# Softmax division folded into the turning of the tiles, output copies on ScalarE, and a new order of three products

## The reference

```python
# layer 2, per image
energy = jnp.einsum('bci,bcj->bij', q, k)
attention = jax.nn.softmax(energy, axis=-1)
out = jnp.einsum('bcj,bij->bci', v, attention)
out = gamma[0] * out + xf
# layer 3, per image: scores of theta and phi over sqrt(c)
attn = jax.nn.softmax(scores, axis=-1)
f = jnp.einsum('nab,nib->nia', attn, g)
f = jnp.einsum('nchw,dc->ndhw', f, conv_w)
# then batch norm of f over all images, and + x
```

## Time and profile before

| what | value |
|---|---|
| median of three runs | 5767.16 us (5764.43 to 5773.0) |
| the profiled execution | 5769.15 us, its span 5767.4 us |
| busy, TensorE | 4678.8 us (81%) |
| busy, VectorE | 5074.8 us (88%) |
| busy, ScalarE | 3719.5 us (64%) |
| busy, GpSimd | 4708.2 us (82%) |
| mean granted TensorE clock | 0.946 of full speed |

### The profile page before, as it was taken

One profiled execution on the slowest core, in us unless ns is written; L12 is line 12 of the kernel. 1 busy time (PEld: TensorE's weight loads), 2 busy tenths in 40 slices (PEclk: granted clock), 3 DMA queues, 4 the chain that ended last, 5 costly groups with the idle time before them and its releaser, 6 DMA issues.

```text
span 5767.4 us, 61917 instructions
## 1 busy us (share of the span) xinstructions
PE 4678.8 (81%) x17331; PEld 2709.8 (47%) x17331; DVE 5074.8 (88%) x5978; ACT 3719.5 (64%) x6077; POOL 4708.2 (82%) x3342
## 2 busy tenths in 40 slices
PE   6568888888888888888888888888888888888771
PEld 6134454445445444544454454445444544544451
DVE  4699999999999999999999999999999999999933
ACT  3466666667666766666666667666666766666633
POOL 0698888898888889888988888888889888888810
PEclk9689999999999999999999999999999999999995
DMA  4465555555655555555655555655555555555527
GB/s 129 181 225 220 216 202 217 220 219 207 220 220 216 207 218 219 211 211 220 223 205 214 221 218 208 220 219 201 215 219 219 207 220 220 219 203 220 213 82 295
DMA packets 199100, 1216.87 MB, mean 211 GB/s; under 512 B 27881, under 2 KB 28657, under 8 KB 67697
## 3 DMA queue, kind: packets, MB, share of 16 engines
q1 hardware_dynamic: 194416, 1196.26, 56.1%
q10 hardware_dynamic: 4352, 16.78, 0.7%
HBM read 1158.43 MB, written 54.53 MB: 210 GB/s over the span
## 4 chain that ended last, share of the span: by engine, by line
PE 42%; DVE 25%; issue 15%; ACT 10%; POOL 6%; DMA 1%; DVEq 0%; SPq 0%; POOLq 0%; ACTq 0%
PE psA L814 14%; PE psE L814 13%; DVE psD L484 9%; DVE hs L488 8%; PE psT L814 6%; PE psT L987 4%; DVE nm L513 4%; ACT p L726 4%; POOL pa L300 3%; PE psY L814 3%; ACT da L680 2%; ACT L649 1%; ACT pt L690 1%; DVE psU L477 1%; POOL pa L306 1%
## 5 line engine op out<-in xcount | busy, mean ns | idle before, releaser
L300 POOL TENSOR_TENSOR pa<-hs,rows_all 128x1024 f32<-128x1024 f32 x1024 | 2411.4, 2355 | 530.6 <-DVE hs L488 529.6
L680 ACT ACTIVATE da<-delta,neg_a 128x512 f32<-128x512 f32 x2048 | 1380.2, 717 | 290.4 <-DVE hs L488 278.3
L484 DVE TENSOR_TENSOR psD<-rows_all,psU 128x512 f32<-128x512 f32 x2048 | 1415.1, 691 | 84.5 <-POOL hlast L304 6.2
L488 DVE TENSOR_TENSOR_SCAN hs<-da,hlast,psD 128x512 f32<-128x512 f32 x1024 | 1310.9, 1280 | 36.3
L306 POOL TENSOR_TENSOR pa<-pa 128x512 f32<-128x512 f32 x1024 | 1299.5, 1269 | 40.1
L488 DVE TENSOR_TENSOR_SCAN hs<-da,psD 128x512 f32<-128x512 f32 x1024 | 1249.5, 1220 | 35.2
L814 PE MATMUL psA<-pt,va 128*128 128x256 f32 x4096 | 947.4, 379 | 1.0 <-DVE x L531 0.6
L726 ACT ACTIVATE p<-psE,nm 128x1024 f32<-128x1024 f32 x512 | 571.2, 1116 | 493.4 <-DVE nm L513 493.4
L814 PEld LDWEIGHTS psA<-pt,va 128*128 128x128 f32 x4096 | 763.2, 190 | 178.8 <-issue 91.5
L513 DVE TENSOR_REDUCE nm<-psE 128x1 f32<-128x1024 f32 x512 | 618.7, 1208 | 216.5 <-PE psE L814 216.1
L690 ACT ACTIVATE pt<-psT 128x512 f32<-128x512 f32 x1024 | 559.0, 596 | 373.1 <-PE psT L987 361.6
(11 more groups left out here) (186 smaller groups left out, 5121.6 us busy)
## 6 DMA issues: line engine op xcount, KB each, us to landing
rows_all<-bc_scratch SPq DMA_DIRECT2D x1024, 1024.0 KB, 4.7
xin<-x SPq DMA_DIRECT2D x40, 512.0 KB, 7.7
xres<-x SPq DMA_DIRECT2D x64, 256.0 KB, 6.2
x_scratch<-x SPq DMA_DIRECT2D x32, 512.0 KB, 4.3
f_scratch<-fa SPq DMA_DIRECT2D x32, 512.0 KB, 6.8
xres<-x SPq DMA_DIRECT2D x8, 512.0 KB, 3.7
x1g<-x SPq DMA_DIRECT2D x8, 512.0 KB, 3.6
fa<-x SPq DMA_DIRECT2D x8, 512.0 KB, 3.6
```

The source lines that it names most:

```text
L300: pool.tensor_tensor(pa[:, k % PROD, :, :], hs[:, sl, :, :], rows_all[:, slot, 2:4, :], ALU.mult).then_inc(S["prod"], 1)
L484: dve.tensor_tensor(psD[:, :], rows_all[:, slot, j, :], psU[:, :], ALU.mult).then_inc(S["dbu_ok"], 1)
L488: dve.tensor_tensor_scan(hs[:, sl, j, :], da[:, sl, j, :], psD[:, :], hlast[:, h, n_:n_ + 1] if ch else 0.0, ALU.mult, ALU.add).then_inc(S ...
L680: act.activation(da[:, k % 2, j, :], delta[:, h, cols(ch)], ACT.Exp, scale=neg_a[:, h, 2 * q + j:2 * q + j + 1]).then_inc(S["da_ok"], 1)
```

## The change

The row sums are inverted tile by tile. ScalarE multiplies `ident` by the reciprocals into `spread`, a diagonal matrix (two buffers), and `turn` becomes 8 products of `p` with `spread` in place of 8 transposes, so that `pt` is already divided. The products with `rinv`, `rb` and VectorE's output work go. Gamma goes into the copy of `va` for m=0. For m=0 one more product per group, `ident` with `x1g`, adds the residual in `psA`. ScalarE copies the output from `psA` to `x2` or `fa`. On VectorE, `scans` is split in two, and the reciprocal stands between the second half's product and its scan. In `ORDER`, "rows" moves behind the energy of r=10 and "steps" ahead of that of r=11.

```diff
@@ -230,12 +230,15 @@
-        RECIP_AT = [10, 12, 15, 18]
+        RECIP_AT = [8, 9, 11, 12, 14, 15, 17, 18]
@@ -496,12 +504,12 @@
-                    for m, gq in groups_at(RECIP_AT, o):
-                        i = NG // 2 * m + gq
-                        pair = slice(GT * (i % 2), GT * (i % 2) + GT)
-                        wait(dve, "p_ok", a, GT * (i + 1))
-                        wait(dve, "av_mm", a, i - 1)
-                        dve.reciprocal(rinv[:, pair], rsum[:, pair]).then_inc(S["rinv_ok"], 1)
+                    for m, t in tiles_at(RECIP_AT, o):
+                        i = TILES * m + t
+                        sl = slice(i % (2 * GT), i % (2 * GT) + 1)
+                        wait(dve, "p_ok", a, i + 1)
+                        wait(dve, "spread_ok", a, i - 2 * GT + 1)
+                        dve.reciprocal(rinv[:, sl], rsum[:, sl]).then_inc(S["rinv_ok"], 1)
@@ -518,22 +526,7 @@
-                        wait(dve, "av_mm", a, i + 1)
-                        wait(dve, "rb_ok", a, i + 1)
-                        if m == 0:
...
-                            dve.scalar_tensor_tensor(out=psA[:, 0:GL], in0=psA[:, 0:GL], scalar=c_gam, in1=rb[:, :],
-                                                     op0=ALU.mult, op1=ALU.mult).then_inc(S["scaled"], 1)
-                            wait(dve, "scaled", a, gq + 1)
-                            dve.tensor_tensor(x2[:, part], psA[:, 0:GL], x1g[:, part], ALU.add).then_inc(S["out_ok"], 1)
-                        else:
...
-                            dve.tensor_tensor(fa[:, part], psA[:, 0:GL], rb[:, :], ALU.mult
-                                              ).then_inc(S["out_ok"], 1)
+                        if m == 1:
                             wait(dve, "out_ok", a, i + 1)
                             dve.bn_stats(bst[:, bass.ds(a, 1), gq, :].rearrange("p a s -> p (a s)"), fa[:, part]
                                          ).then_inc(S["bn_ok"], 1)
@@ -559,7 +551,11 @@
                             if scan:
-                                scans(b, k, 1)
+                                inputs(b, k, 1)
+                            for a, o in now:
+                                normalise(a, o)
+                            if scan:
+                                states(b, k, 1)
@@ -707,7 +703,10 @@
+                    if m == 0:
+                        act.activation(va[:, :, :], split(psT), ACT.Copy, scale=c_gam).then_inc(S["v_ok"], 1)
@@ -722,18 +721,31 @@
+                def spread_out(a, o):
+                    for m, t in tiles_at(RECIP_AT, o):
+                        i = TILES * m + t
+                        rs = i % (2 * GT)
+                        wait(act, "rinv_ok", a, i + 1)
+                        wait(act, "turn", a, 2 * (i - 1))
+                        act.activation(spread[:, i % 2, :], ident[:, :], ACT.Copy, scale=rinv[:, rs:rs + 1]
+                                       ).then_inc(S["spread_ok"], 1)
+
+                def weighed(a, o):
 
                     for m, gq in groups_at(ATTEND_AT, o):
                         i = NG // 2 * m + gq
+                        part = slice(gq * GL, (gq + 1) * GL)
                         wait(act, "av_mm", a, i + 1)
-                        wait(act, "out_ok", a, i)
-                        act.activation(rb[:, :], psA[:, GL:2 * GL], ACT.Copy).then_inc(S["rb_ok"], 1)
+                        if gq == 0:
+                            at(act, ("x2_out", "f_out")[m], a * 16)
+                        if m == 1:
+                            wait(act, "bn_ok", a - 1, gq + 1)
+                        act.activation((x2, fa)[m][:, part], psA[:, 0:GL], ACT.Copy).then_inc(S["out_ok"], 1)
@@ -764,6 +776,7 @@
                             for a, o in now:
+                                spread_out(a, o)
                                 turned_out(a, o)
@@ -969,7 +982,7 @@
-                    wait(pe, "p_ok", a, i + 1)
+                    wait(pe, "spread_ok", a, i + 1)
@@ -984,8 +997,8 @@
-                            last = pe.transpose(psT[:, q, 128 * j:128 * j + 128],
-                                                p[:, i % 2, (4 * q + j) * 128:(4 * q + j + 1) * 128], ident[:, :])
+                            last = mm(psT[:, q, 128 * j:128 * j + 128],
+                                      p[:, i % 2, (4 * q + j) * 128:(4 * q + j + 1) * 128], spread[:, i % 2, :])
@@ -997,13 +1010,12 @@
                     if half:
-                        wait(pe, "rinv_ok", a, i + 1)
-                        for u in range(GT):
-                            rs = (GT * i + u) % (2 * GT)
-                            last = mm(psA[:, GL + 128 * u:GL + 128 * u + 128], rinv[:, rs:rs + 1].to_broadcast([128, 128]),
-                                      ident[:, :])
+                        if m == 0:
+                            wait(pe, "x1g_ok", a, NCH)
+                            last = mm(psA[:, 0:GL], ident[:, :], x1g[:, gq * GL:(gq + 1) * GL], start=False)
@@ -1043,9 +1055,9 @@
-                    "gates add rows",
-                    "energy turn add",
-                    "energy steps add weigh0",
+                    "gates add",
+                    "energy rows turn add",
+                    "steps energy add weigh0",
```

More of the change, by code:

```diff
@@ L122, in build @@
         rsum = sb("rsum", [128, 2 * GT])
-        rb = sb("rb", [128, GL])
+        spread = sb("spread", [128, 2, 128])
         rinv = sb("rinv", [128, 2 * GT])
@@ L182, in build @@
             x1_mm=NCH, x1_ok=NCH, x1g_ok=NCH,
-            rb_ok=NG, q_mm=1, k_mm=2, v_mm=2, q_ok=1, k_ok=2, v_ok=2,
-            e_mm=16, nm_ok=16, p_ok=16, turn=32, pt_ok=32, rinv_ok=NG, av_mm=NG,
-            scaled=NG // 2, out_ok=NG, bn_ok=NG // 2,
+            q_mm=1, k_mm=2, v_mm=2, q_ok=1, k_ok=2, v_ok=2,
+            e_mm=16, nm_ok=16, p_ok=16, turn=32, pt_ok=32, rinv_ok=16, spread_ok=16, av_mm=NG,
+            out_ok=NG, bn_ok=NG // 2,
         )
@@ L232, in build, with tiles_at @@
         TURN_AT = [8, 10, 12, 12, 14, 15, 17, 18]
-        RECIP_AT = [10, 12, 15, 18]
+        RECIP_AT = [8, 9, 11, 12, 14, 15, 17, 18]
         WEIGH_AT = [(11, 12), (14, 15), (17, 18), (19, 19)]
         ATTEND_AT = [13, 16, 18, 20]
+        def tiles_at(table, o):
+            return [(m, t) for m in range(2) for t in range(TILES) if 16 * m + table[t] == o]
         def turned_at(o):
-            return [(m, t) for m in range(2) for t in range(TILES) if 16 * m + TURN_AT[t] == o]
+            return tiles_at(TURN_AT, o)
         def groups_at(table, o):
@@ L468, in normed, with inputs @@
                     dve.tensor_tensor(xn[:, KC - 1 + fc * CH:KC - 1 + fc * CH + CH], xcen[:, :], rstd[:, :], ALU.mult).then_inc(S["xn_ok"], 1)
-                def scans(b, k, j):
+                def inputs(b, k, j):
                     ch, r = divmod(k, NS)
@@ L549, in image @@
                             if scan:
-                                scans(b, k, 0)
+                                inputs(b, k, 0)
+                                states(b, k, 0)
                             if front_of and r == AT_N:
                                 normed(*front_of)
-                            for a, o in now:
-                                normalise(a, o)
                             if att and k == 2:
@@ L709, in value @@
                     wait(act, "v_mm", a, m + 1)
-                    act.activation(va[:, :, :], split(psT), ACT.Copy).then_inc(S["v_ok"], 1)
+                    if m == 0:
+                        act.activation(va[:, :, :], split(psT), ACT.Copy, scale=c_gam).then_inc(S["v_ok"], 1)
+                    else:
+                        act.activation(va[:, :, :], split(psT), ACT.Copy).then_inc(S["v_ok"], 1)
                 def residual(b, ch):
@@ L754, in image @@
                             for a, o in now:
-                                spread(a, o)
+                                weighed(a, o)
                             if att and k == 5:
@@ L999, in values @@
                     for j in range(TB // 2 * half, TB // 2 * (half + 1)):
-                        last = mm(psA[:, 0:GL], va[:, j, :], pt[:, i % 2, j, :], start=(j == 0), stop=(j == TB - 1))
+                        last = mm(psA[:, 0:GL], va[:, j, :], pt[:, i % 2, j, :], start=(j == 0),
+                                  stop=(j == TB - 1 and m == 1))
                     if half:
-                        wait(pe, "rinv_ok", a, i + 1)
-                        for u in range(GT):
-                            rs = (GT * i + u) % (2 * GT)
-                            last = mm(psA[:, GL + 128 * u:GL + 128 * u + 128], rinv[:, rs:rs + 1].to_broadcast([128, 128]),
-                                      ident[:, :])
+                        if m == 0:
+                            wait(pe, "x1g_ok", a, NCH)
+                            last = mm(psA[:, 0:GL], ident[:, :], x1g[:, gq * GL:(gq + 1) * GL], start=False)
                         last.then_inc(S["av_mm"], 1)
```

12 lines of the change are left out of this document (5 added, 7 removed).

## The result

The changed kernel takes 6155.89 us (median of 5 runs, 6152.96 to 6160.08) where the kernel before takes 5767.16 beside it: ratio 1.0674, 95% interval 1.0661 to 1.0687. It is slower by 389 us; the forecast was slower by 216, and 6155.89 lies above its upper end of 6110. The direction was right, the size was not.

What follows compares the result with a forecast made beforehand. TensorE was taken to bound the first stretch, VectorE the third, nobody the second. 2.4 + 1.2 + 3.2 - 0.3 = +6.5 us an image, 202 us over 31, plus 14 for the tail: 5985 us, range 5880 to 6110, 64%.

Steps and rivals of the forecast that it cites:

- What bounds the kernel: Half an image in three stretches: TensorE bounds the first, VectorE the third, nobody the second, where TensorE idles 6.45 us.
- The turn as a product: A tile's turn becomes 16 instructions, about 1.74 us, +0.87 us a tile; TensorE's balance is +12.0 us an image.
- First stretch, the new waits: Last energy to next pass's first: turns 6 and 7 wait 0.75 and 0.8 us; stretches grow 2.4 and 3.2 us.
- ScalarE: Output copy replaces the rb copy at no cost; the new spread takes 0.2 us, 0.35 from its start to TensorE's.
- From the first energy to the last maximum but one: Walk through tiles 0 to 6 of each half: +1.2 us on 50.67 in the first, -0.3 us in the second.
- The move of the three products gains 0.8, not 4.: ORDER's move ends the 2.92 us wait before w_x, but ScalarE is late next, so exponential 2 gains only 0.8 us.
- VectorE's relief is worth nothing.: VectorE's net -4.1 us an image gains nothing; its idle time moves to the maxima of tiles 0, 4 and 6.
- A turn of 3.5 us: Rival: a product with spread costs twice what the rinv row shows, each turn 1.74 us longer again; 6834 us; 2%.
- VectorE's relief wins: Rival: VectorE's third stretch sets the pace, turns 4 to 7 start without a wait; -4.1 us an image, 5643 us; 13%.
- Waits swallow the handoffs: Rival: only work in the saturated stretch counts, 2.5 us an image; 5848 us, about 5781 to 5880; 17%.
- The moved products pay in full: Rival: ending the w_x wait and slow product shortens images by 6.4 us, cancelling 6.5; 5770 us, no change; 4%.
- What would show it.: Signs: turn about 1.75 us, TensorE near 88% busy, no w_x wait, spread waits, VectorE idle some 3 us, image about 172.

Runs made afterwards that it cites:

- e9: Changed kernel with the spread of tile 7 put ahead of the output copy of group 2 on ScalarE: 6089.06 us, 67 under the changed kernel.
- e5: Changed kernel with "steps" put behind energy 3 again, "rows" still moved: 6247.07 us, 91 us slower than the changed kernel.
- e1: Changed kernel with the three strings of ORDER as they were before: 6243.18 us, 87 us slower than the changed kernel.
- e2: Kernel before with only the three new strings of ORDER: 5751.0 us, ratio 0.997 to the kernel before.
- e7: Kernel before with only "rows" moved behind the energy of step 10: 5921.67 us, ratio 1.0271 to the kernel before.
- e8: Changed kernel with 8 transposes a tile waiting for the exponential alone, without reciprocals, spreads and division: 5654.67 us, 112 under the kernel before.
- e4: Changed kernel turning by products with ident, waiting for the exponential alone, without reciprocals, spread copies and division: 5824.37 us, 332 under the changed kernel.
- e12: Kernel before, old order, with two unread products of constants ahead of w_x where TensorE waits for xc: 5689.81 us, ratio 0.9852 to the kernel before.
- e10: Kernel before with the new ORDER and one unread product ahead of "steps": 5751.45 us, ratio 0.997 to the kernel before.
- e11: Changed kernel with both the unread product of e6 and the spread move of e9: 6030.27 us, 126 under the changed kernel.
- e6: Changed kernel with one unread 64x512 product ahead of "steps", where TensorE waits for turn 1's copies: 6102.06 us, 54 us faster than the changed kernel.

## Why the prediction was wrong, point by point

**What bounds the kernel.** Right: the first stretch is TensorE's. Too weak a reading of the second: its 6.45 us of idle TensorE in the earlier trace rows lay ahead of products that were late, so it was no reserve for the longer turns.

**The turn as a product.** Right: 16 instructions, 1.78 us against 1.74; the page's 421 us more are 13.2 us an image for the 12.0 of the balance. The 3.5 us that the prediction drew from two pages of the Trainium skill did not come: 4096 products took two instructions each, 8192 in all, and each of the length of a transpose. The "4 passes" of the Trainium skill (FP8 and Floating Point Precision, TensorE Precision Notes) are not what the trace disagrees with: at 2.4 GHz a product's 0.22 us are some four cycles for each of its 128 columns. The transpose took 0.11 us, some two cycles a column, so it is twice as fast as the product here and not four times.

**First stretch, the new waits.** Right in mechanism and size: 0.77 and 0.76 us against 0.75 and 0.8; the stretch with the x1g products grows by 3.2 us as forecast, the other by 1.6 against 2.4. The 0.8 us that it gives back fit the clock: in the kernel before this stretch stood at 1.2 GHz for 2.0 us in the mean (it fell there in 14 of 24 second halves), up to 1.0 us lost, and in the changed kernel never. The half image that the prediction read, at granted clock 1.00, was one without a fall. e9 shows that the second of the two waits is on the path.

**ScalarE.** The spread's duration is 396 ns, outside both bounds, which were the rb copy's 378 ns above and 148 ns below; the number of columns was a bad measure. From the spread's start to TensorE's it was 0.45 us and not 0.35. At the two places of the first stretch this did not show, since the waits came out as said.

**From the first energy to the last maximum but one: the step that failed.** Turn 0 at 7.01 (7.0), exponential 1 at 9.6 (9.5), exponential 2 at 19.9 (19.9), energy 4 to energy 6 18.2 (18.0), all in first halves: right. Then two steps in a row were not:

1. "Exponential 2 is at 19.9, energy 3 at 21.1." The walk let ScalarE's exponential end the wait and forgot that in the new `ORDER` the products of "steps" stand between. They need `psT`, which the second copy of turn 1 frees just as exponential 2 starts, and then take 1.8 us. Energy 3 is at 22.0 / 22.7: 0.9 + 1.6 us an image. e5, without that neighbour, has it at 21.2 / 21.3.
2. "From energy 3 TensorE runs through ... energy 4 at 32.0." It does run through, but part of it at 1.2 GHz: 12.7 and 12.3 us in place of 10.9 and 10.5, 1.8 + 1.8 us an image. The walk took 1.72 us for the energy from a row at full clock, though the earlier trace rows showed, on the w_x product, what a product behind a wait may take. Where the clock stays up the forecast holds: 10.56 us in five second halves of the changed kernel, 11.0 in 11 first halves of e9. "Steps" at 1.2 GHz (3.10 us) is also why energy 3 is later in second halves than in first.

Together 6.1 us an image, and energy 4 to energy 6 another 0.5; the first stretch gives 0.8 back. (6.1 + 0.5 - 0.8) x 31 = 180 us; the 31 images took 384 us more where 202 were forecast, so 182 were missing. The tail took 6.8 us of its 14.

**"The move of the three products gains 0.8, not 4."** By e1 the move is worth 87 us on the changed kernel, 1.4 us a half image; by e2 16 us on the kernel before. "Rows" alone is +156 us on the kernel before (e7) and +4 on the changed one (e5 against e1); "steps" added to it is -171 and -91. The +4 lies within the spread of the runs. So each size depends on what stands beside it and on where the clock falls: e7 gains 1.9 + 0.8 us an image up to E3 and loses 4.2 + 4.3 behind it, no more than half of its 8.6 + 8.7 us at 1.2 GHz there. None of this was in the walk.

**VectorE's relief is worth nothing.** The trace fits it as long as the turns are long: VectorE idles 3.11 us before maximum 0, as said; no run takes the relief alone away. With short turns and no spread (e8) the rest of the change gives 112 us; how much of it is the relief and how much the missing rinv products was not separated.

**The rivals.** *A turn of 3.5 us* fell with the 1.78 us. *VectorE's relief wins* failed on its own condition, the turns without a wait. *Waits swallow the handoffs* failed: e4 shows 332 us on them and on the copies that make the spread. *The moved products pay in full* failed by e1, which gives the move 2.8 us an image of the 6.4, and by e2.

**What would show it.** Right were the turn, w_x, the waits for the spread and the idle VectorE. TensorE was to be near 88% busy and is at 83%, with an image of 179.5 us where 172 was said. But the 88% did not follow from the prediction's own sum: 4678.8 + 31 x 12.0 + 14 us of 5985 are 85%. And busy time at 1.2 GHz counts as busy, so the share does not tell waiting from work.

## What to carry to other kernels

When a piece is moved ahead of another in an in-order queue, write down what it itself waits for, its output buffer too: "steps" brought the wait for a single `psT` in front of the energy. Ask of each product behind a wait of a microsecond or more at which clock it ran in the trace, and at which it will run in its new place; the 8 to 10 us an image at 1.2 GHz moved from w_x to energy 3 with the wait, and were taken for gone. When an order turns out slower than its waits explain, compare the repeats in which the clock stayed up with those in which it fell: that told here that e7 had no more work, only a lower clock. Before a wait that can't be removed, try a product without a reader and measure it: here it gave 1.5% in one place (e12), 54 us in another, and nothing in a third (e10), and with another edit beside it the fall moved again (e11). And price a longer operation and a new wait together as well as apart, since the two overlapped (501 us, not 628).

## What the runs showed of the hardware

The granted clock fell to half at the same place of nearly every image, after TensorE had idled 1.44 us, although it had been at full speed through waits of 1.70, 0.60 and 0.51 us in the 20 us before. The wait alone does not decide it: the clock stayed up in 5 of 22 second halves, and in 11 of 23 first halves of e9, with the same waits since E0. One product more during the idle time kept it up in 18 of 22 second halves and in no first one (e6), and in 5 of 22 and 15 of 23 when a wait elsewhere was gone (e11). A ScalarE copy of 128 columns with a per-partition scale, SBUF to SBUF, took 396 ns, and one of 256 columns from PSUM to SBUF 378 ns. An fp32 product of 128 columns showed two instructions of 0.11 us each, an fp32 transpose of the same tile one.
